# A graph kernel: Tanh for the gate and a power on GpSimd for the inverse deviation, in one of its stages

## The chip, the cores and the metric

The kernel runs on one core of one Trainium2 chip. Its metric is the device time of one execution in microseconds (us). Three runs of the kernel before took 2034.27, 2040.04 and 2042.52 us; the median is 2040.04 us. The profile shows a fourth execution.

## The reference, cut to what matters

Two graph layers run over 100,000 nodes with 128 features and 25,000 edges. Each is followed by a residual sum and a layer norm.

```python
# layer 0: attention over the edges, then a gate between message and skip path
xm = x @ W_n2m
q, k, v = (xm @ W_q + b_q), (xm @ W_k + b_k), (xm @ W_v + b_v)      # 4 heads of 16
alpha = segment_softmax(sum(q[dst] * (k[src] + ee)) / 4, dst)
out   = segment_sum((v[src] + ee) * alpha, dst)
x_r   = xm @ W_skip + b_skip
beta  = sigmoid(concat([out, x_r, out - x_r]) @ W_beta)
x = layernorm(x + (beta * x_r + (1 - beta) * out) @ W_m2n)
# layer 1: weighted sum of neighbours
agg = segment_sum((x @ w2)[src] * edge_weight, dst)
x = layernorm(x + relu(x @ w1 + agg + b))
# layernorm(x) = (x - mean) / sqrt(var + 1e-5) over the 128 features
```

Only a node that is some edge's destination has a message. For all others `out` is zero in layer 0 and `agg` is zero in layer 1.

## The kernel before, in words

The program is written engine by engine: one instruction stream for each, with semaphores between them set by hand. No planner orders anything; the order of the lines in a stream is the order of issue. It runs five stages one after the other.

1. **The edge-and-dense stage** (function `step_a` of each engine, lines 298 to 316, 425 to 437, 505 to 538, 664 to 696 and 882 to 921), the one that the change touches. It has 196 steps. In step k, GpSimd gathers 128 source rows and 128 destination rows of x (L433, L436), TensorE transposes them (L524, L525) and projects the step before to keys, values and queries (L513 to L516). Beside it the dense half takes 512 nodes, as if they had no message: TensorE computes the skip path and the gate's logit from a transposed copy of x (L531, L534), ScalarE makes exp(-logit), VectorE makes the gate `beta`, adds the gated path to x in `hpre` (L906), and takes mean and variance (L868). ScalarE and VectorE then turn the variance into 1/deviation `rs` and -mean/deviation `nb`, ScalarE scales the rows (L659, four instructions), and SyncE stores them in the table `h_tab` (L253).
2. **The scans** over the edges (L922 to L990), mostly on VectorE.
3. **The correction** (`step_b1`, 98 steps of 256 edges): nodes that do have messages are computed again and scattered over `h_tab` (L454).
4. **The second dense stage** (`step_b2`, 196 steps of 512 nodes): layer 1 without neighbours, while GpSimd gathers `h_tab` rows for all edges (L469).
5. **The last correction** (196 groups of 128 edges in 49 steps, written out without a loop): nodes with neighbours are computed again and scattered into the output (L485).

Rings of four buffers tie the engines together. SyncE's step k, in this order: wait until `hpre` of step k-4 is made, load x for step k; wait until the products of step k-4 are made, load the transposed x; wait until ScalarE has scaled step k-5, store it. GpSimd's gather of step k waits only for TensorE's transposes of step k-4.

ScalarE holds one set of activation functions at a time. Line 641 names the set by hand, once, at the start, and no other line of the kernel names one. The stages after the first use ScalarE for 1/deviation through the helper `inv_std` (L623 to L628), which is called in `step_b1`, in `step_b2` and in the last stage; `step_b1` also uses `exp_minus` (L630 to L634). Both helpers work with the functions Relu, Exp and Ln:

```python
act.activation(log_v, spread, ACT.Ln, bias=eps_c[:, 0:1], scale=per).then_inc(lv_sem, 1)
wait(act, lv_sem, j + 1)
act.activation(r, log_v, ACT.Exp, scale=-0.5).then_inc(rs_sem, 1)
```

Of the kernel before, what the change touches and what calls it, by code (L numbers as in the profile page):

```python
# [8 lines left out]
ALU = mybir.AluOpType  # L9
ACT = mybir.ActivationFunctionType  # L10
AX_X = mybir.AxisListType.X

P = 128
D = 128
# [4 lines left out]
NJ = 4  # L19
GN = NJ * P  # L20
U = 4
EPS = 1e-5
# [7 lines left out]
def wait(eng, sem, value):  # L30

    if not (isinstance(value, int) and value <= 0):
        eng.wait_ge(sem, value)


def live(k, lag, n):

    return not isinstance(k, int) or 0 <= k - lag < n
# [24 lines left out]
def gnn_kernel(nc, x, xT, src, dst, ea, eaT, ew, w_n2mT, w_edgeT, w_q, b_q, w_k, b_k, w_v, b_v,  # L63
# [3 lines left out]
    T = -(-E // (P * U)) * U  # L67
# [17 lines left out]
    with ExitStack() as ctx:  # L85
        def sb(name, shape, dt=F32):
            return ctx.enter_context(nc.sbuf_tensor(name, shape, dt))
# [7 lines left out]
        pd = ctx.enter_context(nc.psum_tensor("pd", [P, 2, NJ, 256], F32))  # L95
# [45 lines left out]
        em = sb("em", [P, 2, NJ])  # L141
        ep = sb("ep", [P, 2, NJ])
        beta = sb("beta", [P, 2, NJ])
        stats = sb("stats", [P, U, NJ // 2, 2, 3])
        lv = sb("lv", [P, U, NJ // 2, 2])
        rs = sb("rs", [P, U, NJ // 2, 2])
# [8 lines left out]
        def mean_of(ju, i):  # L155
            return stats[:, ju, i // 2, i % 2, 1:2]


        ident = sb("ident", [P, P])
        a_kv = sb("a_kv", [P, 2 * DM])  # L160
        a_q = sb("a_q", [P, DM])
# [54 lines left out]
        S = {n: sem(n) for n in (  # L216

            "w_in", "pad_in", "edge_in", "edge_in2", "padded", "id0", "id1", "fills", "gp_fill", "wprod", "wcopy",
            "rows", "r_o", "rows_in", "dsteps", "issued", "drops", "drop_in", "checked", "ordered",
            "g_all", "g_iota", "g_rank", "ranked", "g_one", "g_ea", "g_out", "g_back", "g_turn",  # L220

            "t_a", "xsT_a", "kv_a", "q_a", "v_a", "pr_a", "al_a",
            "mm_d1", "cl_d1", "em_d1", "ep_d1", "be_d1", "pre_d1", "bn_d1", "lv_d1", "rs_d1", "nb_d1", "na_d1",

            "sc", "sc_pe", "sc_act", "sc_pool",

# [135 lines left out]
        def _(gp):  # L362
# [63 lines left out]
            gp.wait_ge(S["dsteps"], 1)  # L426
            top_row = gp.to_reg(N - 1)

            for k in range(T):
                u = k % U  # L430
                if k >= U:
                    gp.wait_ge(S["t_a"], k - U + 1)
                gp.indirect_dma_start(out=ring_a[:, u, :], out_offset=None, in_=x[:, :],  # L433
                                      in_offset=bass.IndirectOffsetOnAxis(ap=gidx[:, k, 0:1], axis=0))\
                    .then_inc(ring["xs_in"][u], 16)
                gp.indirect_dma_start(out=ring_b[:, u, :], out_offset=None, in_=x[:, :],  # L436
                                      in_offset=bass.IndirectOffsetOnAxis(ap=gidx[:, k, 1:2], axis=0))\
                    .then_inc(ring["xd_in"][u], 16)
# [10 lines left out]
            for k in range(T2):  # L449
                u = k % U  # L450
# [13 lines left out]
            for k in range(T + 3):  # L464
                if k < T:
                    u = k % U
# [5 lines left out]
                j = k - 3  # L472
# [157 lines left out]
        def exp_minus(act, e, logit, cl_sem, em_sem, j):  # L630

            act.activation(e, logit, ACT.Relu, bias=top_c[:, 0:1]).then_inc(cl_sem, 1)  # L632
            wait(act, cl_sem, j + 1)
            act.activation(e, e, ACT.Exp, bias=top_c[:, 0:1], scale=-1.0).then_inc(em_sem, 1)  # L634
# [3 lines left out]

        @block.scalar
        def _(act):  # L640
            act.preload_act_table_set("natural_log_exp_and_others")

            act.wait_ge(S["wprod"], 1)
            act.activation(a_kv[:, :], pk[:, 0, 0:2 * DM], ACT.Copy)
# [11 lines left out]
            def scale_rows(ju, n, first=0):  # L656

                for i in range(first, n):
                    ins = act.activation(hout[ju][:, i * D:(i + 1) * D], hpre[:, ju, i * D:(i + 1) * D],  # L659
                                         ACT.Identity, bias=nb_of(ju, i), scale=rs_of(ju, i))  # L660
                return ins

            def step_a(k, u, it):
                if live(k, 1, T):
                    j, ju, _ = back(k, u, it, 1)
                    wait(act, S["kv_a"], j + 1)
                    wait(act, S["pr_a"], j - 1)
                    kv = pk[:, ju % 2, DM:2 * DM].rearrange("p (h c) -> p h c", h=H)
                    vo = val[:, :, :, j] if isinstance(j, int) else \
                        val[:, :, :, bass.ds(j, 1)].rearrange("p h c a -> p h (c a)")  # L670
                    act.activation(vo, kv, ACT.Copy).then_inc(S["v_a"], 1)
                    act.activation(q_sb[:, ju % 2, :], pk[:, ju % 2, 2 * DM:3 * DM], ACT.Copy).then_inc(S["q_a"], 1)
                if live(k, 0, T):
                    wait(act, S["t_a"], k + 1)
                    wait(act, S["kv_a"], k)
                    act.activation((xT_two[:, k:k + 2, :] if isinstance(k, int) else xT_two[:, bass.ds(k, 2), :])
                                   .rearrange("p a n -> p (a n)"), pt[:, u % 2, 0:2 * P], ACT.Copy)\
                        .then_inc(S["xsT_a"], 1)
                    wait(act, S["mm_d1"], k + 1)
                    wait(act, S["pre_d1"], k - 1)  # L680
                    exp_minus(act, em[:, u % 2, :], pd[:, u % 2, :, D], S["cl_d1"], S["em_d1"], k)
                if live(k, 3, T):
                    g, gu, itg = back(k, u, it, 3)
                    wait(act, S["nb_d1"], g + 1)
                    wait(act, ring["h_st"][gu], 16 * itg)
                    scale_rows(gu, NJ - 1)
                if live(k, 1, T):
                    wait(act, S["bn_d1"], j + 1)
                    act.activation(lv[:, ju, :, :], stats[:, ju, :, :, 2], ACT.Ln, bias=eps_c[:, 0:1], scale=1.0 / D)\
                        .then_inc(S["lv_d1"], 1)  # L690
                if live(k, 3, T):
                    scale_rows(gu, NJ, NJ - 1).then_inc(S["na_d1"], 1)
                if live(k, 1, T):
                    wait(act, S["lv_d1"], j + 1)
                    act.activation(rs[:, ju, :, :], lv[:, ju, :, :], ACT.Exp, scale=-0.5).then_inc(S["rs_d1"], 1)
            run_steps(act, T, 3, step_a)


# [68 lines left out]
        def _(dve):  # L767
# [16 lines left out]
            dve.memset(ew_t[:, :], 0.0).then_inc(S["fills"], 1)  # L784
            dve.memset(eps_c[:, :], EPS)
            dve.memset(top_c[:, :], TOP)
            dve.memset(r_o[:, :, :], 0.0)
            dve.memset(pair[:, :, :], 1.0)
            dve.memset(ones3[:, :], 1.0)
# [92 lines left out]
            def step_a(k, u, it):  # L882
                if live(k, 1, T):

                    j, ju, _ = back(k, u, it, 1)
                    wait(dve, S["q_a"], j + 1)
                    dve.scalar_tensor_tensor(out=prod[:, ju % 2, :], in0=pk[:, ju % 2, 0:DM], scalar=QSCALE,
                                             in1=q_sb[:, ju % 2, :], op0=ALU.mult, op1=ALU.mult).then_inc(S["pr_a"], 1)
                if live(k, 0, T):
                    wait(dve, S["em_d1"], k + 1)  # L890
                    dve.tensor_scalar(ep[:, u % 2, :], em[:, u % 2, :], 1.0, None, ALU.add).then_inc(S["ep_d1"], 1)  # L891
                if live(k, 1, T):
                    wait(dve, S["pr_a"], j + 1)
                    ao = alpha[:, :, j:j + 1] if isinstance(j, int) else alpha[:, :, bass.ds(j, 1)]
                    dve.reduce_sum(ao, prod[:, ju % 2, :].rearrange("p (h c) -> p h c", h=H), AX_X)\
                        .then_inc(S["al_a"], 1)
                if live(k, 0, T):
                    wait(dve, S["ep_d1"], k + 1)
                    dve.reciprocal(beta[:, u % 2, :], ep[:, u % 2, :]).then_inc(S["be_d1"], 1)
                if live(k, 0, T):  # L900

                    wait(dve, ring["xg_in"][u], 16 * (it + 1))
                    wait(dve, S["na_d1"], k - U + 1)
                    wait(dve, S["be_d1"], k + 1)
                    for i in range(NJ):
                        ins = dve.scalar_tensor_tensor(  # L906
                            out=hpre[:, u, i * D:(i + 1) * D], in0=pd[:, u % 2, i, 0:D],
                            scalar=beta[:, u % 2, i:i + 1], in1=xg[:, u, i * D:(i + 1) * D],
                            op0=ALU.mult, op1=ALU.add)
                    ins.then_inc(S["pre_d1"], 1)  # L910
                if live(k, 2, T):
                    g, gu, _ = back(k, u, it, 2)
                    wait(dve, S["rs_d1"], g + 1)
                    neg_mean(gu, NJ // 2).then_inc(S["nb_d1"], 1)
                if live(k, 0, T):
                    wait(dve, S["pre_d1"], k + 1)
                    pair_stats(u, NJ // 2).then_inc(S["bn_d1"], 1)
# [232 lines left out]
```

## Time and profile before

| | |
|---|---|
| median of three runs | 2040.04 us |
| the profiled execution's own time | 2031.24 us |
| its span, first to last instruction | 2029.6 us |
| TensorE busy | 1275.5 us (63%) |
| VectorE busy | 1349.0 us (66%) |
| ScalarE busy | 1232.7 us (61%) |
| GpSimd busy | 1043.8 us (51%) |
| moved by DMA | 368.66 MB, mean 182 GB/s |

How to read it: no engine is busy for more than two thirds of the span, but that is a mean over five stages with different limits. The stages stand one after the other, so what an edit is worth has to be read inside the stage in which it acts. The profiled execution took 8.8 us less than the median of the three runs, and sums are made against the profiled one.

### The profile page before, as it was taken

To read this page: it belongs to the slowest core of one execution; us is meant where nothing else is said; L and a number is where in the kernel's file an instruction comes from. 1 tells how busy PE (TensorE), PEld (TensorE's weight loads), DVE (VectorE), ACT (ScalarE), POOL (GpSimd) and SP (SyncE) were. 2 spreads that over 40 slices of the span, in tenths; PEclk is the share of its full clock that TensorE was granted. 3 is DMA by queue.
4 is the path that set the end of the run, shared out by engine and by line. 5 is a ranking of instruction groups with operands and counts; after the bars stand their busy time and mean duration, and the time that the engine had idled before them with its cause. 6 is when DMAs were issued, how large, how long until landed. Compare 5 with 4: busy or idle time off the path is not lost. (4 is left out here: it accounts for less than half of the span.)

```text
span 2029.6 us, 39110 instructions
## 1 busy us (share of the span) xinstructions
PE 1275.5 (63%) x8398; PEld 1085.1 (53%) x8398; DVE 1349.0 (66%) x4876; ACT 1232.7 (61%) x4224; POOL 1043.8 (51%) x1183
## 2 busy tenths in 40 slices
PE   0677777777776720377676747777777775656653
PEld 0666666666665620255454536666666665546543
DVE  1576767767767779755555538888888885545553
ACT  0587888888888840144555438888888994222221
POOL 0555555555555520055545558887884002656655
PEclk9898999989999975688988889999999998787787
DMA  4688888888988830033333338888888773222221
GB/s 146 197 282 257 283 272 276 286 266 284 287 272 268 282 127 0 19 103 106 102 103 99 105 106 230 257 251 254 252 250 248 228 229 116 78 69 79 78 70 46
DMA packets 222282, 368.66 MB, mean 182 GB/s; under 512 B 37380, under 2 KB 81005, under 8 KB 222119
## 3 DMA queue, kind: packets, MB, share of 16 engines
q1 hardware_dynamic: 162625, 255.14, 39.4%
q0 software_dynamic: 31360, 61.17, 12.4%
q10 hardware_dynamic: 28224, 51.39, 6.6%
q8 instruction: 43, 0.70, 0.2%
q14 instruction: 30, 0.25, 0.0%
HBM read 216.45 MB, written 146.43 MB: 179 GB/s over the span
## 5 line engine op out<-in xcount | busy, mean ns | idle before, releaser
L868 DVE BATCH_NORM_STATS2 stats<-hpre 128x6 f32<-128x256 f32 x980 | 376.8, 422 | 3.5
L433 POOL DMA_INDIRECT ring_a<-in_x,gidx x196 | 185.5, 947 | 283.2 <-PE pt L525 229.4
L454 POOL DMA_INDIRECT h_tab<-xg,sidx x196 | 193.3, 986 | 261.1 <-ACT xg L721 202.5
L659 ACT ACTIVATE hout<-hpre,nb,rs 128x128 f32<-128x128 f32 x686 | 291.8, 480 | 0.5 <-DVE hout L878 0.3
L659 ACT ACTIVATE scan_buf<-hpre,nb,rs 128x128 f32<-128x128 f32 x686 | 291.4, 480 | 0.0
L534 PE MATMUL pd<-w_sx,scan_buf 128*128 128x129 f32 x1568 | 241.0, 284 | 0.0
L632 ACT ACTIVATE em<-pd,top_c 128x4 f32<-128x4 f32 (+1 forms) x294 | 76.7, 261 | 269.4 <-PE pd L565 81.5
L906 DVE SCALAR_TENSOR_TENSOR hpre<-pd,beta,xg 128x128 f32<-128x128 f32 x784 | 220.8, 345 | 25.3
L469 POOL DMA_INDIRECT ring_a<-h_tab,gidx x196 | 196.0, 1000 | 58.5 <-POOL big L475 51.8
L534 PEld LDWEIGHTS pd<-w_sx,scan_buf 128*128 128x128 f32 x1568 | 219.6, 202 | 3.9
L575 PE MATMUL pt<-ident,xg 128*128 128x128 f32 x784 | 127.8, 286 | 142.7 <-DMA xg<-h_tab 136.1
L436 POOL DMA_INDIRECT ring_b<-in_x,gidx x196 | 185.4, 946 | 60.5 <-issue 60.5
L584 PEld LDWEIGHTS pk<-w_sb,scan_buf 128*128 128x128 f32 x1568 | 206.7, 192 | 8.5
L485 POOL DMA_INDIRECT out_z<-hout,sidx x100 | 99.6, 996 | 214.0 <-DVE hout L878 181.8
L584 PE MATMUL pk<-w_sb,scan_buf 128*128 128x128 f32 x1568 | 207.2, 275 | 0.0
L531 PE MATMUL pd<-bias,ones 128*128 128x258 bf16 x392 | 113.3, 289 | 148.9 <-DMA scan_buf<-in_xT 117.5
L1058 DVE SCALAR_TENSOR_TENSOR hpre<-pk,xg 128x512 f32<-128x512 f32 x196 | 135.0, 689 | 92.3 <-PE pk L584 62.1
L575 PEld LDWEIGHTS pt<-ident,xg 128*128 128x128 f32 x784 | 84.6, 142 | 173.3 <-DMA xg<-h_tab 92.7
L758 ACT ACTIVATE scan_buf<-pd 128x512 f32<-128x512 f32 x49 | 29.3, 597 | 239.4 <-remote 107.8
L736 ACT ACTIVATE scan_buf<-pt 128x512 f32<-128x512 f32 x196 | 117.0, 597 | 63.7 <-issue 31.6
L891 DVE TENSOR_SCALAR ep<-em 128x4 f32<-128x4 f32 x196 | 36.1, 184 | 173.9 <-ACT em L634 102.4
L513 PE MATMUL pk<-b_kvq,pair 128*128 128x192 f32 x392 | 111.8, 368 | 44.7 <-issue 24.2
(178 smaller groups left out, 3319.2 us busy)
## 6 DMA issues: line engine op xcount, KB each, us to landing
xg<-in_x SPq DMA_DIRECT2D x196, 256.0 KB
scan_buf<-in_xT SPq DMA_DIRECT2D x196, 256.0 KB
xg<-h_tab SPq DMA_DIRECT2D x196, 256.0 KB
h_tab<-hout SPq DMA_DIRECT2D x98, 256.0 KB
h_tab<-scan_buf SPq DMA_DIRECT2D x98, 256.0 KB
out_z<-hout ACTq DMA_DIRECT2D x98, 256.0 KB
out_z<-scan_buf ACTq DMA_DIRECT2D x98, 256.0 KB
xg<-big SPq DMA_DIRECT2D x98, 128.0 KB
```

Source lines behind the costliest of these rows:

```text
L433: gp.indirect_dma_start(out=ring_a[:, u, :], out_offset=None, in_=x[:, :], in_offset=bass.IndirectOffsetOnAxis(ap=gidx[:, k, 0:1], axis=0))\
L436: gp.indirect_dma_start(out=ring_b[:, u, :], out_offset=None, in_=x[:, :], in_offset=bass.IndirectOffsetOnAxis(ap=gidx[:, k, 1:2], axis=0))\
L454: gp.indirect_dma_start(out=h_tab[:, :], out_offset=bass.IndirectOffsetOnAxis(ap=sidx[:, 2 * k + i:2 * k + i + 1], axis=0), in_=hd2[:, u, ...
L469: gp.indirect_dma_start(out=ring_a[:, u, :], out_offset=None, in_=h_tab[:, :], in_offset=bass.IndirectOffsetOnAxis(ap=gidx[:, k, 0:1], axi ...
L534: mm = pe.matmul(pd[:, u % 2, j, 0:D + 1], xgT[:, u, j * P:(j + 1) * P], w_sx[:, 0:D + 1], start=False, stop=j % 2 == 1)
L575: mm = pe.transpose(pt[:, u % 2, j * P:(j + 1) * P], xg[:, u, j * D:(j + 1) * D], ident[:, :])
L584: mm = pe.matmul(pk[:, gu % 2, j * D:(j + 1) * D], xgT[:, gu % 2, j * P:(j + 1) * P], w1_sb[:, :], start=False, stop=j == NJ - 1)
L659: ins = act.activation(hout[ju][:, i * D:(i + 1) * D], hpre[:, ju, i * D:(i + 1) * D], ACT.Identity, bias=nb_of(ju, i), scale=rs_of(ju, i))
L736: act.activation(xgT[:, u % 2, :], pt[:, u % 2, :], ACT.Copy).then_inc(S["hT_d2"], 1)
L868: ins = dve.bn_stats(stats[:, ju, i, :, :].rearrange("p j s -> p (j s)"), two)
L906: ins = dve.scalar_tensor_tensor(out=hpre[:, u, i * D:(i + 1) * D], in0=pd[:, u % 2, i, 0:D], scalar=beta[:, u % 2, i:i + 1], in1=xg[:, u, ...
L1058: dve.scalar_tensor_tensor(out=hpre[:, ju, :], in0=pk[:, ju % 2, :], scalar=0.0, in1=xg[:, ju, :], op0=ALU.max, op1=ALU.add).then_inc(S["u ...
```

## The change: what it does

In `step_a` alone, the gate sigmoid(z) was 1/(1 + exp(-z)): Relu and Exp on ScalarE (`exp_minus`, L681), an addition and a reciprocal on VectorE. It becomes 0.5 + 0.5 tanh(z/2): one Tanh on ScalarE and one VectorE instruction. The inverse deviation was exp(-0.5 ln(v + eps)), with Ln and Exp on ScalarE. Now VectorE makes v + eps and GpSimd raises it to the power -0.5, in the instruction stream that also issues the gathers; its loop becomes four steps longer and has a wait for VectorE ahead of each power. The four scaling instructions of ScalarE stand together. The set that ScalarE is told to load at the start is another one. The other stages' lines are as they were.

```diff
+        half_c = sb("half_c", [P, NJ // 2, 2])
...
-            for k in range(T):
+            for k in range(T + U):
                 u = k % U
+                if k >= U:
+                    j = k - U
+                    gp.wait_ge(S["lv_d1"], j + 1)
+                    gp.tensor_tensor(rs[:, u, :, :], lv[:, u, :, :], half_c[:, :, :], ALU.pow)\
+                        .then_inc(S["rs_d1"], 1)
+                if k >= T:
+                    continue
                 if k >= U:
                     gp.wait_ge(S["t_a"], k - U + 1)
...
-            act.preload_act_table_set("natural_log_exp_and_others")
+            act.preload_act_table_set("exp_and_others")
...
-                    exp_minus(act, em[:, u % 2, :], pd[:, u % 2, :, D], S["cl_d1"], S["em_d1"], k)
+                    act.activation(em[:, u % 2, :], pd[:, u % 2, :, D], ACT.Tanh, scale=0.5).then_inc(S["em_d1"], 1)
                 if live(k, 3, T):
                     g, gu, itg = back(k, u, it, 3)
                     wait(act, S["nb_d1"], g + 1)
                     wait(act, ring["h_st"][gu], 16 * itg)
-                    scale_rows(gu, NJ - 1)
-                if live(k, 1, T):
-                    wait(act, S["bn_d1"], j + 1)
-                    act.activation(lv[:, ju, :, :], stats[:, ju, :, :, 2], ACT.Ln, bias=eps_c[:, 0:1], scale=1.0 / D)\
-                        .then_inc(S["lv_d1"], 1)
-                if live(k, 3, T):
-                    scale_rows(gu, NJ, NJ - 1).then_inc(S["na_d1"], 1)
-                if live(k, 1, T):
-                    wait(act, S["lv_d1"], j + 1)
-                    act.activation(rs[:, ju, :, :], lv[:, ju, :, :], ACT.Exp, scale=-0.5).then_inc(S["rs_d1"], 1)
+                    scale_rows(gu, NJ).then_inc(S["na_d1"], 1)
...
+            dve.memset(half_c[:, :, :], -0.5)
...
-                    dve.tensor_scalar(ep[:, u % 2, :], em[:, u % 2, :], 1.0, None, ALU.add).then_inc(S["ep_d1"], 1)
+                    dve.tensor_scalar(beta[:, u % 2, :], em[:, u % 2, :], 0.5, 0.5, ALU.mult, ALU.add)\
+                        .then_inc(S["be_d1"], 1)
...
-                if live(k, 0, T):
-                    wait(dve, S["ep_d1"], k + 1)
-                    dve.reciprocal(beta[:, u % 2, :], ep[:, u % 2, :]).then_inc(S["be_d1"], 1)
+                if live(k, 1, T):
+                    wait(dve, S["bn_d1"], j + 1)
+                    dve.tensor_scalar(lv[:, ju, :, :], stats[:, ju, :, :, 2], 1.0 / D, EPS, ALU.mult, ALU.add)\
+                        .then_inc(S["lv_d1"], 1)
```

## Rows read from the trace of the kernel before

**Rows 1.** Stretches: PE, PEld, DVE, ACT, POOL busy, clock, DMA share, GB/s.
```profile
61.00:724.00 663.00, 470.40 (x3464) 410.68 (x3464) 474.85 (x2115) 548.90 (x2108) 361.43 (x383) 0.96 0.86 272
858.00:1209.00 351.00, 240.25 (x1022) 172.71 (x1022) 185.23 (x753) 171.43 (x658) 191.58 (x195) 0.89 0.31 103
1213.00:1690.00 477.00, 342.06 (x2551) 302.43 (x2552) 391.95 (x1180) 414.74 (x1176) 276.41 (x392) 0.99 0.83 244
1690.00:2029.60 339.60, 192.91 (x1226) 177.10 (x1226) 169.84 (x540) 72.75 (x196) 194.91 (x196) 0.79 0.23 69
```

**Rows 2.** Groups of ScalarE instructions, whole span: busy us, mean ns, idle before them.
```profile
L626 ACT ACTIVATE lv<-stats,eps_c 128x4 f32<-128x4 f32 (+1 forms) x343 | 98.7, 288 | 7.0 <-DVE stats L868 6.9
L628 ACT ACTIVATE rs<-lv 128x4 f32<-128x4 f32 (+1 forms) x343 | 70.3, 205 | 10.9
L641 ACT ACT_TABLE_LOAD x1 | 1.3, 1283 | 1.0 <-PEq L1143 1.0
```

**Rows 3.** Timeline of ScalarE in the second dense stage: start us, us, instruction.
```profile
1355.05 0.87 ACT L659 ACTIVATE scan_buf<-hpre,nb,rs 128x128 f32<-128x128 f32 x2
1355.82 0.29 ACT L626 ACTIVATE lv<-stats,eps_c 128x4 f32<-128x4 f32 x1
1356.14 0.20 ACT L628 ACTIVATE rs<-lv 128x4 f32<-128x4 f32 x1
1356.28 0.60 ACT L736 ACTIVATE scan_buf<-pt 128x512 f32<-128x512 f32 x1
...
1357.93 0.29 ACT L626 ACTIVATE lv<-stats,eps_c 128x4 f32<-128x4 f32 x1
```

**Rows 4.** Waits of ScalarE in the first correction: us in total, times, longest.
```profile
ACT em L632 <- PE pd L565: 73.7, 35, 4.0
ACT em L632 <- remote: 48.9, 14, 6.1
```

**Rows 5.** Timeline of the last correction, ScalarE and its neighbours, one step.
```profile
1853.17 0.60 ACT L758 ACTIVATE scan_buf<-pd 128x512 f32<-128x512 f32 x1 [3.61 <-issue]
...
1854.14 0.30 ACT L626 ACTIVATE lv<-stats,eps_c 128x4 f32<-128x4 f32 x1
...
1854.71 1.25 DVE L878 TENSOR_SCALAR scan_buf<-hpre,stats,rs 128x128 f32<-128x128 f32 x4 [1.69 <-issue]
...
1857.59 0.66 PE L606 MATMUL pd<-ident,big 128*128 128x128 f32 x4 [2.02 <-issue]
```

**Rows 6.** Timeline of ScalarE in the edge-and-dense stage, where nothing is late.
```profile
303.02 0.28 ACT L689 ACTIVATE lv<-stats,eps_c 128x4 f32<-128x4 f32 x1
...
304.45 0.30 ACT L634 ACTIVATE em<-em,top_c 128x4 f32<-128x4 f32 x1
...
305.81 0.29 ACT L689 ACTIVATE lv<-stats,eps_c 128x4 f32<-128x4 f32 x1
```

**Rows 7.** The longest wait for a transfer in the edge-and-dense stage, 61 to 724 us.
```profile
PEld pd L531 <- DMA scan_buf<-in_xT: 153.8, 143, 2.3
```

**Rows 8.** Timeline of ScalarE in the first correction.
```profile
1007.17 0.26 ACT L632 ACTIVATE em<-pd,top_c 128x2 f32<-128x2 f32 x1 [0.23 <-PE pd L565]
...
1008.77 0.28 ACT L707 ACTIVATE ring_b<-pt 128x128 f32<-128x128 f32 x1
```

**Rows 9.** The stretch of that stage with the highest DMA share.
```profile
520.00:540.00 20.00, 14.39 (x112) 12.32 (x111) 15.79 (x71) 18.13 (x71) 11.58 (x14) 1.00 0.92 287
```

**Rows 10.** Groups on GpSimd, second dense stage, 1216 to 1560 us.
```profile
L475 POOL TENSOR_TENSOR big<-ring_a,ew_t 128x128 f32<-128x128 f32 x196 | 81.1, 414 | 6.6 <-DMA ring_a<-h_tab,gidx 2.5
```

**Rows 11.** Timeline: the first gathers and the transpose that waits for them.
```profile
50.18 0.96 POOL L436 DMA_INDIRECT ring_b<-in_x,gidx  x1 [0.30 <-issue]
...
54.55 0.45 PE L524 MATMUL pt<-ident,ring_b 128*128 128x128 f32 x1 [39.20 <-DMA ring_b<-in_x,gidx]
```

**Rows 12.** Timeline from a step's transposes to its reciprocal, edge-and-dense stage.
```profile
305.14 0.28 PE L524 MATMUL pt<-ident,ring_b 128*128 128x128 f32 x1
...
307.81 0.17 DVE L899 RECIPROCAL beta<-ep 128x4 f32<-128x4 f32 x1
```

More of the change, by code:

```diff
@@ L222, in gnn_kernel @@
             "t_a", "xsT_a", "kv_a", "q_a", "v_a", "pr_a", "al_a",
-            "mm_d1", "cl_d1", "em_d1", "ep_d1", "be_d1", "pre_d1", "bn_d1", "lv_d1", "rs_d1", "nb_d1", "na_d1",
+            "mm_d1", "em_d1", "be_d1", "pre_d1", "bn_d1", "lv_d1", "rs_d1", "nb_d1", "na_d1",
             "sc", "sc_pe", "sc_act", "sc_pool",
```

## The prediction

> **What bounds the kernel now.** I read the stages first, because the page's shares are means. The stretches [rows 1] give four: the edge-and-dense stage 663 us for 196 steps, or 3.38 us a step; the first correction 351 us for 98 steps, 3.58; the second dense stage 477 us for 196, 2.43; the last correction 340 us for 49, 6.93. What is left is start-up and the scans, which use neither a gate nor a deviation.
>
> Then the groups of ScalarE [rows 2]. The Ln and Exp of the helper (L626, L628) run 343 times each: 98 in the first correction, 196 in the second dense stage, 49 in the last correction. They are not in the edit and stay. One row more matters: in 2030 us the activation tables are loaded once, at line 641, in 1283 ns. One set serves everything. It is named by hand, after the natural logarithm and the exponential.
>
> Next, what limits each stage. In the second dense stage ScalarE is busy 415 of 477 us, and where nothing is late the Ln instructions start 2.11 us apart (1355.82 to 1357.93) [rows 1, 3]: ScalarE is all but its bound. In the first correction ScalarE is busy 171 of 351 us; it waits for TensorE's products (73.7 us) and for something outside the engines (48.9 us) [rows 1, 4]. In the last correction the timeline [rows 5] is a ring: two copies on ScalarE, Ln, Exp, VectorE's normalisation, its next sums, TensorE's transposes at 1857.59, and then the next copies, which need those transposes. Here the Ln and Exp are on the path although ScalarE is busy for only 73 of 340 us. In the edge-and-dense stage ScalarE's clean step is 2.79 us (303.02 to 305.81) [rows 6], under the 3.38 that a step takes; the difference is mostly the wait for the transposed x, 153.8 us in 143 waits, with the DMA engines at a share of 0.86 [rows 1, 7].
>
> **The change, part by part.**
>
> *The set of tables.* The new name at line 641 is that of the exponential's set. The edited stage has Tanh and copies, and one name can serve it. But Ln comes back 343 times later on, each time with an Exp behind it. I take it that the program places a load in front of every activation whose function the active set lacks, and that it takes the first set that has this function, without looking ahead. Then Ln brings a set in which Exp is missing, Exp brings the first set back, and each pair costs two loads: 2 x 343 = 686. No row shows such a pair, and that this is how sets are chosen is my assumption; the first rival drops it. What speaks for it: the kernel before names a set by hand, and of the joint set (it has "natural_log_exp" in its name) one load serves both.
>
> The Trainium skill, "ScalarE: Activation LUTs", section "Table sets: the hidden batching unit", lists exp and tanh in the one set, exp and ln together in the other. So it agrees that Ln has to be fetched; it does not list the set that a lone Ln gets.
>
> *The price of a pair.* Two loads of 1.283 us [rows 2] are 2.57. A load also keeps its neighbours from overlapping: the two row scalings end at 1355.92 and Ln starts at 1355.82; Exp ends at 1356.34 and the next copy starts at 1356.28 [rows 3]. I lose the 0.10 and add 0.03 for each load, the gap between Ln's end (1356.11) and Exp's start (1356.14): 2.73 us. The lower bound is 2.57. Above, no row bounds the emptying of the engine around a load; the nearest is that same gap, and if one whole activation of 0.29 had to drain at each load, it would be 3.1.
>
> The Trainium skill, same page, section "What ACT_TABLE_LOAD costs", has 1283 ns, as the row here, and about 1380 ns of drain beside it. By that a switch is 2.66 us and the pair 5.3; this is the second rival.
>
> *Second dense stage.* The clean step 2.11 becomes 2.11 + 2.73 = 4.84 us; transposes, products and transfers of a step fit beside it (they fit in 2.43 now). 196 x 4.84 = 949, less 477: **+472 us**. Bounds: +2.57 on the clean step and not a moment idle gives +440; 3.1 on top of the present 2.43 gives +608. I take the clean step, since the idle time of now is waiting for transfers that then have twice the time.
>
> *First correction.* From the gate (1007.17) to the next step's copy (1008.77) is 1.60 us, and that copy takes about 0.2 before the next can start: 1.80 [rows 8]. With the pair 4.53, for 98 steps 444, less 351: +93. The waits for products are covered, as those are started a ScalarE step earlier. The waits of 48.9 us that no engine ends may stay. I take most of them: **+125 us**. Bounds: +93, and +268 if no idle time at all is absorbed (98 x 2.73).
>
> *Last correction.* Ln and Exp are in the ring, so the pair is paid in full: 49 x 2.73 = **+134 us**. It is less where the ring stands for another reason (clean, from 1853.17 to some 1858.4, it is 5.2 us, against 6.93 on the mean), so the lower bound is half, +67, and the upper 49 x 3.1 = +152. I take +130.
>
> *Edge-and-dense stage, ScalarE.* Each step loses an Exp of 0.30 (L634), a Ln of 0.28 (L689) and the Exp of the deviation, 0.2 as in [rows 3]: the clean step goes from 2.79 to about 2.0 us [rows 6]. It was not the bound. But SyncE's queue waits for the scaled rows before it issues the next loads, and they are ready about 0.6 us earlier. What can be won is the DMA engines' idle time: at the best share of the stage, 0.92 [rows 9], instead of 0.86 a step is 3.38 x 0.86/0.92 = 3.16, -43 us in all. The other bound is zero.
>
> *The same stage, VectorE.* Two small instructions for the gate become one, and one for v + eps comes in: no change in number.
>
> *The same stage, GpSimd.* The power has no row. The nearest is the product of 128 x 128 elements, 0.41 us [rows 10]; this one has four per partition, so I take 0.4, with bounds of 0.1 and 1.3. What counts is what is queued behind it. The gathers of step k now stand behind the power of step k-4, which needs VectorE in step k-3, and not only behind TensorE's transposes of step k-4. They are issued more than a step later. The new ring spans three steps: power 0.4 with its gap 0.3; first gather 0.95 and gap 0.3; the second gather until it is used, 50.18 to 54.55 or 4.4 [rows 11]; from the transposes to where v + eps will stand, 305.14 to 307.98 or 2.8, less the Exp's 0.3 [rows 12]. That is 8.9, or 3.0 us a step, below 3.38. If a gather takes 2 us longer under full load, it is 10.9, or 3.6: +49 us; with a power of 1.3 us too it is 3.9, +110. For the stage I take **-15 us**.
>
> **Sum**, against the profiled execution's own 2031.24 us: + 472 + 125 + 130 - 15 = +712, so 2743. The median of the runs is 8.8 higher; I forecast **2750 us**.
>
> **The rivals.**
>
> *A: the program looks ahead.* Where Ln is needed first, it picks the set that also holds Exp. Then one load of 1.3 us ends the matter and the three large terms vanish: 2031 - 15 + 1 + 9 = 2026 us, not slower. It decides at one place, the first L626 of the first correction. For it: before the change all loops live on one load [rows 2]. Against it: that load was named by hand, and this change names another. The Trainium skill, "ScalarE activation tables: per-element evaluation and per-set limits", section "Table sets in the compiler and the runtime", speaks for it: loads are placed per block by the greedy longest run of activations. The one load of before fits this as well as mine. Chance 0.08.
>
> *B: each switch costs as much again.* 686 x 1.3 = +890, 3640 us. For it is only the page's drain; here Exp follows Ln with a gap of 0.03 us although it needs its result, so the engine drains fast [rows 3]. Chance 0.07.
>
> *C: the gathers become the bound* of the edge-and-dense stage. At 3.9 us a step it costs +110 and not -15: 2875 us. For it: the new ring has only 0.4 us a step to spare, and its transfers meet a DMA share of 0.86. Against it: the sum stays below. Chance 0.12.
>
> **How the numbers follow.** The forecast has 0.73. Its own ends are +440 + 93 + 67 - 43 and +608 + 268 + 152 + 49, or 2597 and 3117 us; ends all on one side are unlikely, and I give 2640 to 2960 as the range, which takes in C. A and B lie outside with 0.15. A measurement of this kernel tells about 0.5%, 10 us. Only A is not slower: its 2026 is 0.7% below 2040, so faster gets 0.04, same 0.03, slower 0.93.
>
> **What would show it.** Right: some 687 ACT_TABLE_LOAD rows, two for each L626/L628 pair of now, 1.28 us each; ScalarE near 100% busy in the second dense stage with Ln starts 4.8 us apart; the first correction near 475 us; the last near 470; the edge-and-dense stage at 3.3 us a step, with TensorE's transposes not waiting for gathers. Wrong: one or two loads in the whole trace (A); gaps over 1 us beside the loads (B); transposes waiting for ring_b in step after step (C). Should the last correction grow by less than 67 us, its ring is not what I take it for.

## The result

The changed kernel took 2687.09 us (median of 4 runs, 2683.04 to 2691.52), the kernel before 2039.43 us beside it (4 runs). The ratio is 1.318, with a 95% interval of 1.3145 to 1.3214: slower by a third. The forecast was 2750 us. The profiled execution took 2683.04 us, with a span of 2681.2 us.

The stages are cut at the first ScalarE instruction of each, in both traces:

| stage | before | after | difference | forecast |
|---|---|---|---|---|
| edge-and-dense (L676, now L684; first to last) | 672.9 | 702.6 | +30 | -15 |
| scans | 114.6 | 114.5 | 0 | 0 |
| first correction | 372.9 | 460.4 | +88 | +125 |
| second dense stage | 477.4 | 942.0 | +465 | +472 |
| last correction | 336.6 | 406.1 | +70 | +130 |

The stretches of the changed kernel, in the columns of [rows 1] (engine busy us, TensorE's granted clock, DMA share, GB/s). The four are the edge-and-dense stage, the first correction, the second dense stage and the last correction.

```profile
61.00:758.00 697.00, 490.51 (x3487) 455.99 (x3486) 465.42 (x2131) 438.54 (x1543) 580.43 (x578) 0.91 0.82 260
872.70:1333.10 460.40, 286.51 (x1083) 193.97 (x1083) 197.05 (x783) 427.35 (x882) 193.30 (x199) 0.83 0.25 81
1333.10:2275.10 942.00, 504.47 (x2557) 427.33 (x2556) 413.76 (x1191) 922.39 (x1569) 271.71 (x390) 0.72 0.40 123
2275.10:2681.20 406.10, 229.61 (x1217) 211.36 (x1215) 165.78 (x531) 203.58 (x294) 191.89 (x196) 0.74 0.19 57
```

ScalarE, the fourth number, is busy for 922 of the 942 us of the second dense stage. In the first stretch it is GpSimd, the fifth number, that went from 361 of 663 to 580 of 697 us.

The page of the changed kernel, its costliest groups, in answer to [rows 2] (columns: xcount | busy us, mean ns | idle before):

```profile
L634 ACT ACT_TABLE_LOAD x343 | 440.1, 1283 | 6.2 <-issue 0.2
L636 ACT ACT_TABLE_LOAD x343 | 440.1, 1283 | 6.1
...
L435 POOL TENSOR_TENSOR rs<-lv,half_c 128x4 f32<-128x4 f32 x196 | 204.6, 1044 | 27.7 <-DVE lv L900 20.3
```

Line 634 is the helper's Ln and 636 its Exp. In front of each of their 343 executions stands a table load of 1283 ns; with the one at the start that makes 687. They are busy for 880 us. And the power on four elements per partition takes 1.04 us.

One step of ScalarE in the second dense stage of the changed kernel (start us, us), against [rows 3]:

```profile
1802.14 1.25 ACT L667 ACTIVATE hout<-hpre,nb,rs 128x128 f32<-128x128 f32 x3
1803.41 1.28 ACT L634 ACT_TABLE_LOAD   x1
1804.70 0.30 ACT L634 ACTIVATE lv<-stats,eps_c 128x4 f32<-128x4 f32 x1
1805.02 1.28 ACT L636 ACT_TABLE_LOAD   x1
1806.31 0.20 ACT L636 ACTIVATE rs<-lv 128x4 f32<-128x4 f32 x1
1806.42 0.58 ACT L735 ACTIVATE scan_buf<-pt 128x512 f32<-128x512 f32 x1
...
1808.17 1.28 ACT L634 ACT_TABLE_LOAD   x1
```

No gap is over 0.02 us, and the step is 4.76 us (1803.41 to 1808.17) where it was 2.11: the pair of loads costs 2.65. The Trainium skill ("ScalarE: Activation LUTs", section "What ACT_TABLE_LOAD costs") adds some 1380 ns of drain to each load; the load's 1283 ns are as it says, the drain isn't there: the scaling ends at 1803.39 and the load starts at 1803.41, and Ln starts 0.01 us after the load has ended.

GpSimd in the edge-and-dense stage of the changed kernel:

```profile
310.31 1.04 POOL L435 TENSOR_TENSOR rs<-lv,half_c 128x4 f32<-128x4 f32 x1
311.54 1.02 POOL L441 DMA_INDIRECT ring_a<-in_x,gidx  x1 [0.19 <-issue]
312.86 0.95 POOL L444 DMA_INDIRECT ring_b<-in_x,gidx  x1 [0.30 <-issue]
313.84 1.04 POOL L435 TENSOR_TENSOR rs<-lv,half_c 128x4 f32<-128x4 f32 x1
```

One follows the other with no wait for anybody: a power, two gathers, 3.53 us a step (310.31 to 313.84). The stage's mean is 702.6 / 196 = 3.58. GpSimd is its bound. TensorE now waits in front of the transposes of the gathered rows, which it did not do before the change in this stage:

```profile
PE pt L532 <- issue: 169.7, 108, 3.7
```

That is 169.7 us in 108 waits between 61 and 758 us. The profile names no releaser there ("issue").

### The profile page after: what moved, and what is told of

Its sections match the earlier page's. It is cut to its first block, busy times and chain, and to the rows that moved or that the text cites. A ratio compares the mean times of both kernels' runs of the same rounds, so it can differ in the third digit from the quotient of the medians.

```text
span 2681.2 us, 39405 instructions
## 1 busy us (share of the span) xinstructions
PE 1524.6 (57%) x8398; PEld 1298.8 (48%) x8398; DVE 1357.7 (51%) x4877; ACT 2004.4 (75%) x4322; POOL 1254.6 (47%) x1379
## 4 chain that ended last, share of the span: by engine, by line
ACT 29%; issue 17%; ACTq 1%; PE 1%; POOL 1%; DVE 1%; POOLq 0%; DVEq 0%
ACT L634 11%; ACT scan_buf L667 4%; ACT hout L667 4%; ACT lv L634 3%; ACT scan_buf L735 2%; ACT L636 2%; ACT scan_buf L757 1%; ACTq L254 1%; ACT scan_buf L758 1%; ACT rs L636 1%; POOL out_z L493 1%; ACTq L33 0%; PE pd L614 0%; DVE big L1091 0%; ACTq L56 0%
## 5 line engine op out<-in xcount | busy, mean ns | idle before, releaser
L634 ACT ACT_TABLE_LOAD x343 | 440.1, 1283 | 6.2 <-issue 0.2
L636 ACT ACT_TABLE_LOAD x343 | 440.1, 1283 | 6.1
L589 PE MATMUL pk<-bias,ones 128*128 128x512 bf16 x196 | 95.4, 487 | 422.7 <-ACT scan_buf L735 401.5
L873 DVE SCALAR_TENSOR_TENSOR nb<-stats,rs 128x4 f32<-128x4 f32 (+1 forms) x490 | 81.3, 166 | 497.7 <-ACT rs L636 362.7
L592 PEld LDWEIGHTS pk<-w_sb,scan_buf 128*128 128x128 f32 x1568 | 301.0, 269 | 11.4
L592 PE MATMUL pk<-w_sb,scan_buf 128*128 128x128 f32 x1568 | 304.4, 359 | 0.0
L542 PE MATMUL pd<-w_sx,scan_buf 128*128 128x129 f32 x1568 | 258.0, 297 | 0.0
L589 PEld LDWEIGHTS pk<-bias,ones 128*128 128x128 bf16 x196 | 19.5, 99 | 487.2 <-ACT scan_buf L735 345.6
L542 PEld LDWEIGHTS pd<-w_sx,scan_buf 128*128 128x128 f32 x1568 | 234.1, 214 | 7.6
L435 POOL TENSOR_TENSOR rs<-lv,half_c 128x4 f32<-128x4 f32 x196 | 204.6, 1044 | 27.7 <-DVE lv L900 20.3
L583 PE MATMUL pt<-ident,xg 128*128 128x128 f32 x784 | 176.2, 369 | 18.3 <-DMA xg<-h_tab 18.3
L532 PE MATMUL pt<-ident,ring_b 128*128 128x128 f32 x196 | 61.6, 314 | 216.7 <-issue 169.7
```

Of the source, the lines that this page charges most:

```text
L435: gp.tensor_tensor(rs[:, u, :, :], lv[:, u, :, :], half_c[:, :, :], ALU.pow)\
L542: mm = pe.matmul(pd[:, u % 2, j, 0:D + 1], xgT[:, u, j * P:(j + 1) * P], w_sx[:, 0:D + 1], start=False, stop=j % 2 == 1)
L592: mm = pe.matmul(pk[:, gu % 2, j * D:(j + 1) * D], xgT[:, gu % 2, j * P:(j + 1) * P], w1_sb[:, :], start=False, stop=j == NJ - 1)
```

## The experiments

The ratios are taken against the kernel before on the same chip. The runs lie on three chips: e1 to e4, e5 to e8, and e9 to e11. The kernel before took 1877 to 1879 us beside the first eight and 1873 us beside the last three, where it had taken 2039 us beside the changed kernel; what that is became a question of its own (e7, e8, e11). Stage times are cut as in the table above and come from one traced execution each; those of the kernel before are e7's and e11's, so for e1 to e4 they are from another chip. With the same code in the edge-and-dense stage, the traces of the changed kernel, e1, e5, e6 and e8 have 700.2 to 712.7 us for it, and those of e7, e9 and e11 658.7 to 665.0: differences of a few microseconds between two traces say nothing.

**e1: the joint set, once.** Added to the changed kernel:

```diff
+            act.preload_act_table_set("natural_log_exp_and_others")
             act.wait_ge(S["sc"], 3)
             act.activation(decay[:, :, :], decay[:, :, :], ACT.Exp).then_inc(S["sc_act"], 1)
```

> One line is added to the changed kernel: ScalarE is told to load the joint set (natural logarithm and exponential) once, between the edge-and-dense stage and the scans. Theory 'loads': the changed kernel's 648 us over the one before are 686 table loads in the three later stages (first correction +88, second dense stage +465, last correction +70, 622 in all by the traces) and +30 in the edge-and-dense stage. So this runs in 2687 - 622 = 2065 us, with 2 table loads in the trace and the later stages as long as before. Rival 'spill-over': the later stages are longer for another reason too, such as TensorE's lower granted clock (0.72 in the second dense stage) or GpSimd's new work; then it stays above 2150.

Measured: 1918.33 us, ratio 1.023 (1.020 to 1.026), two loads at the start and between the stages:

```profile
L649 ACT ACT_TABLE_LOAD x1 | 1.3, 1283 | 1.0 <-PEq L1146 1.0
L698 ACT ACT_TABLE_LOAD x1 | 1.3, 1283 | 0.0
```

The three later stages take 294.0, 477.7 and 275.7 us, as those of the kernel before do in e7. So one line takes the ratio from 1.429 (e8) to 1.023, and the rival "spill-over" is out. The 2065 us that were expected missed by the difference between the chips; against the kernel before it is +41 us where +26 were expected, since the edge-and-dense stage of that kernel is shorter there too (659.0 to 665.0 us against e1's 700.2).

**e2: the power left out.** As e1, and in place of the power a product on VectorE. The kernel leaves out the power, so its deviations are not the reference's.

```diff
-                    gp.wait_ge(S["lv_d1"], j + 1)
-                    gp.tensor_tensor(rs[:, u, :, :], lv[:, u, :, :], half_c[:, :, :], ALU.pow)\
-                        .then_inc(S["rs_d1"], 1)
...
+                if live(k, 1, T):
+                    wait(dve, S["lv_d1"], j + 1)
+                    dve.tensor_scalar(rs[:, ju, :, :], lv[:, ju, :, :], -0.5, None, ALU.mult).then_inc(S["rs_d1"], 1)
```

> As the first, with the power left out: VectorE writes a product with -0.5 in place of the power (so the deviations are not the reference's), and GpSimd's stream is that of the kernel before. It tells what the relief of ScalarE alone is worth. Theory 'transfers': the edge-and-dense stage was bound by its transfers at 3.38 us a step, with the DMA engines at a share of 0.86; at the best share seen, 0.92, it is 3.16. So between 1996 and 2035 us, ScalarE's clean step at about 2.0 us. Rival 'ScalarE was the bound there': a step falls by the whole 0.77 us that ScalarE loses, to 2.6, and the time to about 1890.

Measured: 1855.74 us, ratio 0.988 (0.9865 to 0.9904). The edge-and-dense stage takes 643.8 us, 3.28 a step, against 659.0 and 665.0 before (e7, e11). So all that ScalarE's relief is worth, if the deviation cost next to nothing, is 15 to 21 us there; the medians are 21 us apart. That lies in the 4 to 43 us that theory "transfers" asked for, and far from the 150 of its rival. Over 61 to 690 us the stage looks like this, first e2, then the kernel before on such a chip (e7):

```profile
61.00:690.00 629.00, 458.87 (x3429) 411.78 (x3428) 458.82 (x2286) 417.11 (x1520) 360.63 (x382) 0.95 0.89 285
```
```profile
61.00:690.00 629.00, 446.96 (x3349) 387.53 (x3347) 460.73 (x2051) 531.51 (x2042) 354.56 (x376) 0.98 0.88 278
```

ScalarE falls from 532 to 417 us busy and the DMA share only goes from 0.88 to 0.89. TensorE's weight loads still wait for the transposed x, 201.1 us in 150 waits in e2 and 182.8 in 166 in e7.

**e3: a product on GpSimd.** As e1, with `ALU.mult` for `ALU.pow` and nothing else. Here too the power is left out.

> As the first, with a product by -0.5 in place of the power on GpSimd (so the deviations are not the reference's): same stream, same waits, same order, a shorter instruction. Theory 'GpSimd is full': in the changed kernel power 1.04 us, gathers 1.02 and 0.95, gaps 0.51, together 3.52 us, which is the step. With a product of 0.1 to 0.3 us the sum is 2.6 to 2.8, GpSimd is no longer full, and the stage goes back to 3.2 to 3.4 us a step: 2000 to 2035 us. Rival 'late gathers': what costs is that the gathers stand behind VectorE's work of a later step; then the step falls only by a third of what the instruction loses, 0.27 us, to 3.3: 2010 us. The two are near each other here; the next run tells them apart.

Measured: 1864.97 us, ratio 0.994 (0.9922 to 0.9955); the stage takes 644.4 us, as in e2. GpSimd:

```profile
311.83 0.20 POOL L435 TENSOR_TENSOR rs<-lv,half_c 128x4 f32<-128x4 f32 x1 [0.38 <-DVE lv L901]
312.17 0.96 POOL L441 DMA_INDIRECT ring_a<-in_x,gidx  x1
313.43 0.94 POOL L444 DMA_INDIRECT ring_b<-in_x,gidx  x1 [0.30 <-issue]
315.21 0.20 POOL L435 TENSOR_TENSOR rs<-lv,half_c 128x4 f32<-128x4 f32 x1 [0.83 <-DVE lv L901]
```

The product takes 0.20 us, and now GpSimd waits for VectorE in front of it. The queue, the wait and the order are those of the changed kernel, and in this stage they cost 0.6 us against e2, whose gathers stand behind nothing but the transposes. The medians of the two kernels are 9 us apart, which leaves some 9 us for them at most. The power's length is what made the stage 56 us longer in e1.

**e4: the power behind the gathers.** As e1, with GpSimd's stream in this order:

```diff
-            for k in range(T + U):
+            for k in range(T + U + 1):
...
+                if k < T:
+                    if k >= U:
+                        gp.wait_ge(S["t_a"], k - U + 1)
...
+                if k > U:
+                    j = k - U - 1
+                    gp.wait_ge(S["lv_d1"], j + 1)
+                    gp.tensor_tensor(rs[:, j % U, :, :], lv[:, j % U, :, :], half_c[:, :, :], ALU.pow)\
+                        .then_inc(S["rs_d1"], 1)
```

> As the first, but in GpSimd's stream the gathers of step k stand first, behind TensorE's transposes alone as in the kernel before, and then comes the power of step k-5. Theory 'GpSimd is full': the same instructions make the same 3.5 us, so nothing changes against the first run, 2065 us within 10. Rival 'late gathers': the gathers are as early as before, the stage goes back to 3.38 us a step or below, 2035 us or less.

Measured: 1899.88 us, ratio 1.011 (1.0089 to 1.014); the stage takes 683.1 us, 3.49 a step. It stays above the 3.38 a step, 663 us, that "late gathers" asked for, and 17 us below e1, more than the 10 that "GpSimd is full" allowed; neither theory alone has it. The period of its stream is the same 3.52 us (311.21 to 314.73). What went are the steps in which GpSimd had to wait for VectorE ahead of a power; in e1 these waits were

```profile
POOL rs L435 <- DVE lv L901: 20.3, 19, 2.3
```

and in e4 there are 4.3 us of them. The stream of e4:

```profile
311.21 1.04 POOL L444 TENSOR_TENSOR rs<-lv,half_c 128x4 f32<-128x4 f32 x1
312.45 1.02 POOL L435 DMA_INDIRECT ring_a<-in_x,gidx  x1 [0.19 <-PE pt L531]
313.77 0.95 POOL L438 DMA_INDIRECT ring_b<-in_x,gidx  x1 [0.30 <-issue]
314.73 1.05 POOL L444 TENSOR_TENSOR rs<-lv,half_c 128x4 f32<-128x4 f32 x1
```

**e5: the loads in the last correction alone.** As e1, and ahead of that stage `act.preload_act_table_set("exp_and_others")`.

> The first experiment's kernel, but the exponential's set is loaded again ahead of the last correction, so the pairs of table loads come back in that stage alone: 98 of them, 2.73 us a step. Where its traces show no 'remote' waits on ScalarE and VectorE (as in the first four experiments, last correction 274 to 276 us), theory 'ring' expects the whole price, 49 x 2.73 = +134 us in that stage, about 409 us. Rival 'slack': the last correction has room for a part of the loads, as the +70 us of the changed kernel against the one before (337 to 406 us) would have it; then +70 here too, 345 us.

Measured: 2049.10 us, ratio 1.090 (1.0873 to 1.0919). The last correction takes 404.4 us against e1's 275.7, +129, or 2.63 a step. The whole price is paid, and the 345 us of the rival "slack" are out.

**e6: pauses instead of loads.** As e1, in the last correction:

```diff
-                    inv_std(act, stats[:, j % U, :, :, 2], 1.0 / D, lv[:, j % U, :, :], rs[:, j % U, :, :],
-                            S["bn_c"], S["lv_c"], S["rs_c"], j)
...
+                    act.activation(idle_t, idle_t, ACT.Copy)
+                    act.activation(lv[:, j4, :, :], stats[:, j4, :, :, 2], ACT.Ln, bias=eps_c[:, 0:1], scale=1.0 / D)\
+                        .then_inc(S["lv_c"], 1)
...
+                    act.activation(idle_t, idle_t, ACT.Copy)
+                    act.activation(rs[:, j4, :, :], lv[:, j4, :, :], ACT.Exp, scale=-0.5).then_inc(S["rs_c"], 1)
```

> As e5, but instead of each table load ScalarE makes a copy of 1312 elements in place, which reads and writes a buffer that nobody needs by then and takes about 1.28 us; no table is switched. Theory 'time on the ring': what counts is ScalarE's time alone, so the last correction comes out as in e5 within 15 us. Rival 'switching costs more than its row': the kernel of e5 is slower than this one by more than 30 us in that stage.

Measured: 2033.68 us, ratio 1.082 (1.0795 to 1.0848); the stage takes 389.8 us, +114, or 2.33 a step. That is 15 us less than e5, half of the 30 that the rival asked for. ScalarE in e6, then in e5:

```profile
1905.71 0.59 ACT L759 ACTIVATE scan_buf<-pd 128x512 f32<-128x512 f32 x1
1906.19 1.30 ACT L764 ACTIVATE val<-val 128x1312 f32<-128x1312 f32 x1
1907.38 0.30 ACT L765 ACTIVATE lv<-stats,eps_c 128x4 f32<-128x4 f32 x1
...
1908.91 0.19 ACT L769 ACTIVATE rs<-lv 128x4 f32<-128x4 f32 x1
```
```profile
1902.35 0.59 ACT L760 ACTIVATE scan_buf<-pd 128x512 f32<-128x512 f32 x1
1902.95 1.28 ACT L634 ACT_TABLE_LOAD   x1
1904.25 0.30 ACT L634 ACTIVATE lv<-stats,eps_c 128x4 f32<-128x4 f32 x1
...
1905.86 0.20 ACT L636 ACTIVATE rs<-lv 128x4 f32<-128x4 f32 x1
```

A copy lets the next instruction start 1.19 us after its own start, a load 1.30. From the start of the copy ahead of the pair to the start of Exp it is 3.20 us in e6 (1905.71 to 1908.91) and 3.51 in e5 (1902.35 to 1905.86). That overlap makes the 0.3 us a step. A load costs its own time on ScalarE and the overlap of its neighbours, and nothing more.

**e7 and e11: the kernel before, once more, with a trace.**

> The kernel before, unchanged, for its stages on this chip. Its median was 1877 us beside the first four experiments, against 2039 us in the first comparison. Theory 'stops': the difference is the waits that the first trace calls 'remote' and that no engine ends; they are missing here, and the first correction takes 294 and the last 275 us, as in the first experiment. Then the edge-and-dense stage, the scans and the second dense stage are as in the first trace: 673, 115 and 477 us within 15 each. Rival: the difference is in the transfers, and the second dense stage or the edge-and-dense stage is shorter by 50 us or more.

> The kernel before once more, to know which kind of chip these runs are on: with 'remote' waits 2030 to 2045 us and 373 and 337 us in the two corrections, without them 1870 to 1885 us and 294 and 276. No theory of the time ranks between the two; what is asked is whether both corrections always move together.

Measured, one execution each: 1877.65 and 1874.49 us. Their stages: 659.0 and 665.0, 114.7 and 114.7, 294.2 and 294.1, 476.6 and 470.1, 276.4 and 274.3 us. Against the first trace the two corrections lose 79 and 60 us, the edge-and-dense stage 8 to 14, and the others next to nothing. So theory "stops" holds, and in both runs the two corrections moved together. The waits of ScalarE and VectorE that ended with nothing the profile could name (it prints "remote") are gone. In the first trace of the kernel before they were:

```profile
ACT scan_buf L758 <- remote: 107.8, 14, 9.0
ACT em L632 <- remote: 60.7, 18, 6.1
DVE hpre L1098 <- remote: 19.0, 9, 3.7
```

Of the 60.7 us, 48.9 are in the first correction [rows 4] and 11.8 in the edge-and-dense stage. The other two lines are in the last correction. TensorE's granted clock in that stage is nearly the same, 0.79 in the first trace and 0.81 in e7.

**e8: the changed kernel, once more.**

> The changed kernel, unchanged, on this chip. Theory 'stops are covered': the changed kernel had no 'remote' waits in the first comparison, so it is no faster here: 2660 to 2690 us, and its difference to the kernel before on the same chip is about 800 us if that one takes 1877, with +166 in the first correction, +464 in the second dense stage, +131 in the last. Rival: the stops were a fixed cost of both kernels; then this one is faster here by the same 160 us, 2525 us.

Measured: 2689.20 us, ratio 1.429 (1.4247 to 1.4336). Stages 712.7, 114.5, 466.8, 942.0, 406.2 us. The changed kernel takes the same time in both places, just inside the 2660 to 2690 us of the theory and far from the rival's 2525, and in neither trace does it have those waits.

**e9: a short pause.** The kernel before, with one copy of 512 elements ahead of the Ln in the last correction.

> The kernel before, with one copy of 512 elements (0.60 us, some 0.5 from start to start) on ScalarE ahead of each Ln of the last correction, in a buffer that nobody needs by then. Theory 'ring': without 'remote' waits the stage goes from 276 by 49 x 0.5 = +25 us to about 301. Should they be there (the kernel before beside it then takes about 2040 and not 1877 us), it tells whether a pause of this size covers them: stage below 337 us if it does, about 361 if they come on top. Rival: the stage has room for 0.5 us a step, +0.

Measured: 1896.18 us, ratio 1.013 (1.0094 to 1.0161). The stage takes 297.0 us against 274.3 (e11) and 276.4 (e7), +21 to +23, or 0.42 to 0.46 us a step. The unnamed waits were not there, so whether a pause covers them was not tested.

**e10: the power alone.** The changed kernel with the old gate (`exp_minus`, sum and reciprocal) and the joint set from the start.

> One part of the change by itself: the inverse deviation by the power on GpSimd, but the gate as before (Relu, Exp, sum, reciprocal), so the joint set can stay for the whole kernel and is loaded once. Theory 'GpSimd is full': the edge-and-dense stage comes out as in the first experiment, 700 us within 10, since GpSimd's 3.52 us a step is the limit and ScalarE has room either way; against the kernel before, 659 on a chip without 'remote' waits, that is +41 us, a ratio of 1.022. Rival 'the gate by Tanh pays for a part of it': this one is slower than the first experiment by more than 10 us, ratio above 1.027.

Measured: 1922.08 us, ratio 1.026 (1.0228 to 1.0292); the stage takes 700.6 us, e1's 700.2. Against e11 on the same chip the stage is 36 us longer. The ratio lies below the rival's 1.027, but its interval reaches beyond it. With GpSimd full, the Tanh's effect is too small to be seen here.

## Why the prediction was right, and where its terms were off

The forecast was 2750 us, the measured time 2687, and the cause is the forecast one. The nearness of the total is in part luck. Against the profiled execution of before, +712 us were forecast and +652 came: the first and the last correction were 37 and 60 us too high, the edge-and-dense stage 45 us too low. Where the kernel before takes 1879 us, the same change costs 810 us (e8).

*The set.* Right in the trace: two loads at each Ln and Exp pair, and e1 shows that they are the loss. The Trainium skill says that loads are placed per block by the greedy longest run of activations ("ScalarE activation tables: per-element evaluation and per-set limits", section "Table sets in the compiler and the runtime"). That isn't what happened here: rival A needed one load after the first, and there are 686. When the set is named by hand the same instructions need none. Which set each load brings, no row shows.

*The price of a pair.* 2.73 us was forecast, 2.65 measured in the second dense stage and 2.63 in the last correction (e5). Rival B is out.

*Second dense stage.* +472 forecast, +465 measured, +465 again in e8 against e7 (942.0 to 476.6). ScalarE became the only bound, as the clean step of [rows 3] said. TensorE's granted clock fell from 0.99 to 0.72 in that stage; its products (L584, now L592) take 359 ns instead of 275, but stay beside the loads.

*First correction.* +125 forecast, +88 measured. The term took most of the 48.9 us of waits of [rows 4] as staying; they went. Its other part is off as well. The stretch of 351 us that was taken for 98 steps holds 658 of the stage's 686 ScalarE instructions, which is 94 steps; against the stage's 372.9 us the 444 us of the clean sum are +71 and not +93, and the step came out at 4.70 us, not 4.53. On a chip without the waits the stage goes from 294.2 to 466.8 us, or +173: the clean stage has 3.0 us a step and not the 1.80 that ScalarE needs, and 1.76 of the 2.65 are added to it.

*Last correction.* +130 forecast, +70 measured. That is 3 us from the +67 below which the prediction would have called its ring wrong. The ring of [rows 5] is right all the same: e5, e6 and e9 add 2.63, 2.33 and 0.42 to 0.46 us a step for pairs of loads, pairs of long copies and a short one. What was off is the reference: 337 us held some 60 us of the unnamed waits, and the changed kernel doesn't have them. 276.4 to 406.2 is +130, the term as forecast. The prediction had seen that 6.93 us a step stood against a clean 5.2, and took no consequence from it but a lower bound.

*Edge-and-dense stage.* -15 forecast, +30 measured, and here the reasoning failed too. Rival C's sign came: TensorE's transposes wait step after step (169.7 us in 108 waits). But its price of +110 did not, and its mechanism is the smaller part. It looked at how late the gathers are issued, with a ring of three steps, and the power, taken at 0.4 us, takes 1.04. The term that decides was not there: GpSimd's own sum for a step. At the upper bound that the prediction gave for the power, 1.3 us, the sum of 1.3 + 0.95 + 0.95 and gaps is 3.7 us, above the 3.38 of a step (672.9 / 196 = 3.43, with the whole stage counted); it was never made. e3 shows that the order costs next to nothing when the instruction is short, e4 that it is worth 17 of e1's 41 us once GpSimd is full.

*The relief of ScalarE.* Bounds of 0 and -43 us were given, -15 to -21 us measured (e2 against e7 and e11). The waits of TensorE and the DMA share of 0.89 speak for the transfers as the limit of that stage; no run changed them.

*What stays open.* The unnamed waits of the kernel before, some 140 us in the two corrections. They were there in the first comparison and not on the three chips of the experiments; the changed kernel had none in its two traces. They are regular: in the first trace of before, the starts of L758 in the last correction stand 5.1, 5.6 and 9.5 us apart, over and over, and in e7 5.1 us apart in nearly every step. Whether the chip, or the pace of the kernel on it, brings them, no run here tells. The kernel before is 160 us faster without them and the changed kernel is not, so the same change costs a ratio of 1.32 there and 1.43 here. No version with the power beats the kernel before: the best, e4, is at 1.011, and with a product in place of the power (e2) the gain ends at 1.2%. A power on VectorE was not run.

## What to carry to other kernels

Before a function moves to another table set, go through every later use of ScalarE in the program: here a pair of functions that no longer shared a set cost two loads of 1.28 us each time it ran, and naming the joint set once at the border of the stages cost one. When work is moved to an engine that looks half idle, add its new instruction to all that it issues in one step and compare the sum with the step, before thinking of latencies. A stage whose mean step stands well above its clean step has waits that may vanish for other reasons, and a difference taken against it holds only where those waits are.

## What the runs showed of the hardware

- A power of 128 x 4 elements on GpSimd takes 1.04 us, a product of the same shape in the same place 0.20 us (e3), a product of 128 x 128 elements 0.41 [rows 10].
- Behind the power the first gather takes 1.02 us instead of the 0.96 that it takes behind the product.
- A table load lets nothing overlap, but has no other cost outside its 1283 ns: gaps of 0.01 to 0.02 us on both sides. A pair of loads costs 0.3 us more than a pair of copies of 1.30 us, which overlap their neighbours (e5, e6).
